# Two attentions and an expert FFN with adaptive norms: projections cut into halves spread over the steps, Newton steps and scaling of the norms moved to GpSimd, a gelu table load set ahead

## Chip, cores and metric

One core of a Trainium2 chip. The metric is the device time in microseconds of one execution of the program. One execution was also profiled; durations, waits and rows below are of that one.

## What is computed

For 8 batches of 512 tokens of 256 features, in float32:

```python
mod = (silu(c) @ wmod).reshape(8, 6, 1, 256)      # sa, ca, ga, sb, cb, gb
ga = sign(ga) * max(|ga|, 0.25); gb = sign(gb) * max(|gb|, 0.25)
h = layernorm(x) * (1 + ca) + sa
x = x + ga * attn(h)          # 16 heads of 16, causal, softmax, output projection
h = layernorm(x) * (1 + cb) + sb
# FFN: xn = layernorm(h) * ln_g + ln_b
#      o = attention(xn)      # 32 heads of 8, not causal, and wo, plus h
#      y = gelu(o_e @ w1[e] + b1[e]) @ w2[e] + b2[e]   # 256 tokens for each of 2 experts a batch
x = x + gb * y
```

## The kernel before, in words

Each batch b passes a first attention (a = 0, 16 heads, causal) and a second one (a = 1, 32 heads, all keys), then two experts (j = 0, 1). A step works on a group of four heads and one tile of 128 keys: 16 steps for the first attention, 32 for the second. In a step (`scores`, L1056) TensorE makes four score tiles of up to 128 x 512, in two pairs, each pair on two halves of its rows; ScalarE takes their exp into `probs` (L852); for the first attention GpSimd sets what the causal mask excludes to zero (L761); then `values` (L1073) multiplies with v into the bank `out`, one step behind. The maxima of the rows come from a second set of the same products, made 8 steps ahead (`maxima`, L1027), reduced by VectorE (L1263 causal, L1266). After four steps of them, `max_rows` turns 16 rows of maxima (L1036), VectorE negates them, GpSimd splits them into three bf16 parts (L743 to L750), and SyncE writes these as extra rows of `q_stack` (L648), so that the score products subtract the maxima themselves. After four steps of values ScalarE copies the sums out (L868), and `normalise` transposes and divides them (L1082, L1286, L1289).

Beside the steps run the other parts of the batches. `layernorm` has three instances: n = 0 of x, n = 1 of x after the first attention, n = 2 of the FFN's input. Each is cut into 17 pieces on VectorE: statistics, twelve small steps of an inverse root on 128 x 4 (`inverse_root`, three of them a first guess, nine Newton steps, L1195 to L1199), and scaling (L1226). `to_features` (L968) transposes into `act_T`. `v` (L1003), `qk` (L990) and `attention_out` (L1118) are projections in float32. A `qk` item fills the bank `side` with 512 tokens; ScalarE copies it as bf16 (L818), VectorE takes the remainder (L1252), GpSimd splits that again (L725, L727), SyncE stores the slices to HBM (L619), and `stacks` loads them as `q_stack` and `k_stack` (L639). `ffn_sum` (L1128) is the second attention's output, `expert_in` (L1147) and `expert_out` (L1163) are the products of an expert, with gelu between (L888). `bias_part` scales the expert's bias and adds it to x for the residual (L795, L800).

The order on each engine is written out by hand. `sections()` gives a list of items for a start, a section before the loop (batch 0 and the first attention of batch 1), a loop of six turns, and a section after it. One turn has 32 steps of the second attention of batch b, then 16 of the first attention of batch b + 2. `attention()` puts the step's own items in a fixed order; every step has four slots, and `beside` maps a slot number to the side items that are put there. In the loop `n1 = 128` is the first slot of the 16 last steps. Each engine walks the same list, in order, and executes its share; a TensorE item that wants a bank waits until its last fill is drained. There are three banks for scores, three for maxima, one `out` and one `side`, which all projections, transposes and turned maxima share.

```python
place_together(beside, (39, 43), v_items(0, 2))
place_together(beside, (47, 51, 55, 59), qk_items(0, 2))
```

So at slot 47 of a turn the items of a whole `qk` product (two products of 512 columns) follow the second pair of step 11.

## Time and profile before

| what | us |
|---|---|
| median of the runs (3) | 1860.25 |
| lowest and highest run | 1859.96, 1870.94 |
| the profiled execution, its own time | 1867.02 |
| its span from first to last instruction | 1865.3 |

The profiled execution is one of its own, 6.8 us above the median. Durations of rows below belong to it. PE is TensorE, PEld its weight loads, DVE VectorE, ACT ScalarE, POOL GpSimd, SP SyncE. A row of a timeline gives start, length, engine, line, instruction, tiles, count, and in brackets the idle time of the engine before it and what ended that. Float32 products are two instructions each in the trace.

### The profile page before, as it was taken

Reading aid. Unit: us, or ns where it says so; the run is one execution under the profiler, and the core shown is the slowest. Engines: PE = TensorE matmul, PEld = TensorE weight load, DVE = VectorE, ACT = ScalarE, POOL = GpSimd, SP = SyncE. Lnnn points to the kernel's source line nnn. Section 1 sums busy time; section 2 is a strip of 40 time slices with the busy share of each in tenths; the row PEclk is TensorE's granted clock in tenths of the full one; section 3 lists DMA queues with packets and bytes.
Section 4 is the critical chain, followed back from the end, with each engine's and each line's share of the span. In section 5 each row is a group of like instructions: output and inputs, shape, how many; then the busy total and the mean of one; then the engine's idle time right before and its main releaser. Section 6 shows DMA issues by size and latency. Waiting matters only on the chain.

```text
span 1865.3 us, 29184 instructions
## 1 busy us (share of the span) xinstructions
PE 1514.1 (81%) x9745; PEld 632.6 (34%) x9745; DVE 1178.4 (63%) x3109; ACT 985.2 (53%) x1967; POOL 447.5 (24%) x797
## 2 busy tenths in 40 slices
PE   4368759898888888898888888898798887878777
PEld 2123213235323353234332353234432353213315
DVE  3456468863786548864687639864688637775440
ACT  0035326664466546664556546664556545566471
POOL 0132422231322222321222312321222312210100
PEclk8679869999999999999999999999999999999999
DMA  6632152342335223442324324342423422121301
GB/s 173 166 109 42 59 146 59 92 128 71 92 100 120 75 68 110 117 126 71 95 84 101 93 72 123 109 117 64 120 66 99 114 72 82 50 78 43 108 1 57
DMA packets 137263, 171.19 MB, mean 92 GB/s; under 512 B 16984, under 2 KB 102808, under 8 KB 137120
## 3 DMA queue, kind: packets, MB, share of 16 engines
q1 hardware_dynamic: 137120, 169.33, 33.1%
q8 instruction: 84, 1.38, 0.3%
q14 instruction: 59, 0.48, 0.1%
HBM read 110.67 MB, written 56.66 MB: 90 GB/s over the span
## 4 chain that ended last, share of the span: by engine, by line
PE 55%; DVE 21%; ACT 8%; DMA 6%; issue 5%; POOL 3%; SPq 2%; POOLq 0%; ACTq 0%; DVEq 0%
DVE neg_max L1266 12%; PE bank_out L1073 11%; PE bank_scores L1056 8%; PE bank_side L990 7%; PE bank_side L1163 7%; PE bank_max L1027 6%; ACT probs L852 4%; PE bank_side L1003 4%; PE bank_side L1147 3%; PE bank_scores L1147 3%; DMA q_stack<-max_parts 2%; PE bank_side L1082 2%; PE bank_side L1128 2%; DMA b_bc<-in_L_ffn_b_dram 1%; DVE normed L1226 1%
## 5 line engine op out<-in xcount | busy, mean ns | idle before, releaser
L852 ACT ACTIVATE probs<-bank_scores 128x512 f32<-128x512 f32 (+3 forms) x1536 | 751.9, 544 | 513.5 <-PE bank_scores L1056 502.4
L1266 DVE TENSOR_REDUCE neg_max<-bank_max 128x1 f32<-128x512 f32 x1024 | 653.4, 682 | 157.0 <-PE bank_max L1027 153.5
L1056 PE MATMUL bank_scores<-q_stack,k_stack 64*128 64x512 bf16 (+3 forms) x2048 | 323.0, 351 | 154.4 <-ACT probs L852 114.1
L1027 PE MATMUL bank_max<-k_stack,q_stack 64*128 64x512 bf16 (+3 forms) x2048 | 324.4, 352 | 97.1 <-DVE neg_max L1266 55.3
L1073 PE MATMUL bank_out<-probs,v_tile 128*9 128x512 f32 (+4 forms) x3072 | 369.7, 554 | 3.7 <-POOL probs L761 1.5
L1263 DVE CUSTOM_DVE_ANT_0 bank_max<-bank_max,causal 128x384 f32<-128x384 f32 (+3 forms) x512 | 241.7, 515 | 124.2 <-PE bank_max L1027 121.1
L1056 PEld LDWEIGHTS bank_scores<-q_stack,k_stack 64*128 64x128 bf16 x2048 | 86.7, 94 | 484.7 <-issue 434.8
L1027 PEld LDWEIGHTS bank_max<-k_stack,q_stack 64*128 64x128 bf16 x2048 | 105.3, 95 | 203.1 <-issue 126.8
L761 POOL TENSOR_SCALAR_AFFINE_SELECT probs<-probs 128x512 f32<-128x512 f32 x128 | 80.9, 632 | 343.7 <-ACT probs L852 343.7
L743 POOL CAST max_parts<-max_row 16x128 bf16<-16x128 f32 x96 | 26.8, 279 | 564.2 <-DVE max_row L1277 564.2
L1163 PE MATMUL bank_side<-w_out,hidden_T 128*128 128x256 f32 x512 | 130.4, 412 | 3.0 <-DVE y_out L1321 1.0
L1321 DVE TENSOR_TENSOR y_out<-bank_side,gb_bc 128x256 f32<-128x256 f32 x32 | 13.6, 425 | 170.9 <-PE bank_side L1163 170.9
L1163 PEld LDWEIGHTS bank_side<-w_out,hidden_T 128*128 128x128 f32 x512 | 102.8, 206 | 37.5 <-DVE max_row L1277 11.0
L1073 PEld LDWEIGHTS bank_out<-probs,v_tile 128*9 128x9 f32 (+1 forms) x3072 | 47.8, 91 | 118.9 <-issue 100.1
L725 POOL CAST partsq<-rest 128x512 bf16<-128x512 f32 x32 | 19.5, 609 | 233.7 <-DVE rest L1252 233.7
L868 ACT ACTIVATE out_raw<-bank_out 128x512 f32<-128x512 f32 x96 | 57.6, 600 | 31.1 <-PE bank_out L1073 30.3
L1003 PE MATMUL bank_side<-wv,act_T 128*128 128x256 f32 x256 | 68.8, 415 | 5.6 <-DVE max_row L1277 2.2
L1263 DVE DVE_READ_ACCUMULATOR2_ANT neg_max<- 128x1 f32 x512 | 72.4, 141 | 0.0
L990 PE MATMUL bank_side<-act_T,wk 128*128 128x512 f32 x128 | 63.5, 618 | 9.1 <-DVE rest L1252 4.0
L990 PE MATMUL bank_side<-act_T,wq 128*128 128x512 f32 x128 | 67.1, 649 | 2.4 <-DVE rest L1252 1.4
L1082 PE MATMUL bank_side<-ident,out_raw 128*128 128x128 f32 x384 | 63.2, 288 | 4.1 <-DVE expert_xT L1314 1.4
L1082 PEld LDWEIGHTS bank_side<-ident,out_raw 128*128 128x128 f32 x384 | 40.8, 142 | 71.0 <-issue 69.4
(113 smaller groups left out, 1405.5 us busy)
## 6 DMA issues: line engine op xcount, KB each, us to landing
q_stack<-q_parts SPq DMA_DIRECT2D x128, 256.0 KB, 4.8
k_stack<-k_parts SPq DMA_DIRECT2D x128, 192.0 KB, 6.7
w_in<-in_L_ffn_w_dram SPq DMA_DIRECT2D x16, 1024.0 KB, 5.8
w_out<-in_L_ffn_w_dram SPq DMA_DIRECT2D x16, 1024.0 KB, 8.2
q_parts<-partsq SPq DMA_DIRECT2D x32, 384.0 KB, 2.6
k_parts<-partsk SPq DMA_DIRECT2D x32, 384.0 KB, 2.6
q_parts<-partsq SPq DMA_DIRECT2D x32, 256.0 KB, 2.9
k_parts<-partsk SPq DMA_DIRECT2D x32, 256.0 KB, 2.9
```

Source lines behind the costliest of these rows:

```text
L761: pool.affine_select(out=tile, in_=tile, compare_op=ALU.is_ge, fill=0.0, base=0, pattern=[[0, GROUP], [1, P]], channel_multiplier=-1).then ...
L852: nc.scalar.activation(probs[s % 2][:, head_at(k), q0:S], region[bank][:, q0:S], ACT.Exp, scale=float(WIDTH[a]) ** -0.5).then_inc(drained[ ...
L990: ins = pe.matmul(region[bank], w_qkv[a][t][:, cc, oc * P:(oc + 1) * P], act_T[:, cc, :], start=(cc == 0), stop=(cc == C - 1))
L1003: ins = pe.matmul(region[bank][:, k * D:(k + 1) * D], act_T[:, cc, t * P:(t + 1) * P], w_qkv[a][2][:, cc, :], start=(cc == 0), stop=(cc == ...
L1027: ins = pe.matmul(region[to][:, 0:keys], q_stack[buf][rows, at, qt * P:(qt + 1) * P], k_stack[buf][rows, at, 0:keys], start=(i == 0), stop ...
L1056: ins = pe.matmul(region[to][:, q0:S], k_stack[buf][rows, at, kt * P:(kt + 1) * P], q_stack[buf][rows, at, q0:S], start=(i == 0), stop=last)
L1073: ins = pe.matmul(outb[32 * k:32 * k + WIDTH[a] + 1, q0:S], v_tile[a][:, kt, g * GROUP + k, :], probs[s % 2][:, k, q0:S], start=(kt == 0), ...
L1082: ins = pe.transpose(side[:, t * P:(t + 1) * P], out_raw[:, g % 2, t * P:(t + 1) * P], ident[:, :])
L1147: ins = pe.matmul(region[bank][:, k * EXP_TOK:(k + 1) * EXP_TOK], w_in[:, cc, ft * P:(ft + 1) * P], expert_xT[:, cc, j * EXP_TOK:(j + 1) * ...
L1163: ins = pe.matmul(region[bank][:, 0:D], hidden_T[:, ft, k * P:(k + 1) * P], w_out[:, ft, :], start=(ft == 0), stop=(ft == FT - 1))
L1263: v.tensor_tensor_reduce(region[bank][:, 0:keys], region[bank][:, 0:keys], causal[:, S - keys:S], 1.0, -3e38, ALU.add, ALU.max, dst).then_ ...
L1266: v.tensor_reduce(dst, region[bank], AX_X, ALU.max).then_inc(drained[bank], 1)
```

## The change

`qk`, `v` and `attention_out` become items of half the size (256 columns of q or k, one tile of 128 tokens of v or of the output), each a fill of `side` of its own, with its copy, remainder, split and add in halves too. In the loop and the section after it they are placed one to a step; in the section before the loop mostly two at one place. Stores to HBM stay whole. VectorE keeps the statistics and the three steps of the first guess; GpSimd does thirteen steps of Newton's method on 128 x 4 (four kinds where VectorE had three, and one that scales by -0.5), and the scaling of 128 x 256 tiles. The copy of the value sums is an item of its own (`sums_out`), half a step later. `bias_part` moves from slot 2 to slot 7. The first `expert_out` item of each expert is placed before the second pair of scores of its step instead of behind it. A new item `gelu_table` computes a gelu of one column, placed ahead of the expert's products. Slots of norms, transposes, stack loads and FFN inputs are moved too.

```diff
-PIECES = {"qk": 2, "v": 2, "attention_out": 2, "ffn_sum": 2, "expert_in": 2, "expert_out": 4}
+PIECES = {"ffn_sum": 2, "expert_in": 2, "expert_out": 4}
...
+            if s % T_STEPS == T_STEPS - 1:
+                half = p * 2 + 2 + VALUES_SLOT[a] // 2 + 1
+                waiting.setdefault((half // 2, half % 2 * 2 + 1), []).append(("sums_out", *main[p]))
...
 def place_experts(plan, off, at):
...
         items = plan.setdefault(start, [])
+        items.append(("gelu_table", off, j))
...
-        place_together(plan, (start + SLOTS, start + 2 * SLOTS), [("expert_out", off, j, k) for k in range(2)])
+        place_at(plan, (start + 2, start + 2 * SLOTS), [("expert_out", off, j, k) for k in range(2)])
...
-    place_layernorm(beside, 82, 0, 1, 4)
+    place_layernorm(beside, 82, 0, 1, 2)
...
-    place_together(beside, (98, 100), v_items(1, 0))
-    place_together(beside, (103, 106, 109, 112), qk_items(1, 0))
+    place_at(beside, (98, 98, 100, 100), v_items(1, 0))
+    place_at(beside, (103, 103, 106, 106, 109, 109, 111, 111), qk_items(1, 0))
...
-    place(beside, 2, [("bias_part", 0, 0), ("bias_columns", 0)])
+    place(beside, 7, [("bias_part", 0, 0), ("bias_columns", 0)])
...
+    place(beside, 12, layernorm_items(2, 0), 2)
+    place_at(beside, (15, 17, 19, 23), out_items(1))
+    place_at(beside, (29, 33), features_items(2, 0))
+    place_at(beside, range(35, 67, 4), qk_items(0, 2))
+    place_at(beside, range(67, 83, 4), v_items(0, 2))
...
+    place(beside, 30, layernorm_items(1, 1), 3)
+    place(beside, 70, layernorm_items(1, 2), 2)
+    place_at(beside, (91, 93), features_items(1, 2))
+    place_at(beside, (95, 97, 99, 103), v_items(1, 1))
+    place_at(beside, range(107, 139, 4), qk_items(1, 1))
...
-    place(beside, n1 + 7, [("stacks", 1, 2), ("keep_v", 1)])
+    place(beside, n1 + 7, [("keep_v", 1)])
+    place(beside, n1 + 18, [("stacks", 1, 2)])
...
+            def layernorm(b, f, n, piece):
+
+                src = (x_in, x1, ffn_x)[n]
+                dst = normed[n % 2]
+                if piece < NEWTON_PIECE:
+                    return
+                if piece == NEWTON_PIECE:
+                    for step in range(GUESS_STEPS, ROOT_STEPS):
+                        newton_step(b, n, step)
+                    return
+                half = piece - NEWTON_PIECE - 1
+                if half == 0:
+                    wait(pool, rstd_made[n], ROOT_STEPS * (b + 1))
+                    for user in ((0, 2), (1,), (0, 2))[n]:
+                        if user in turned_fill:
+                            bank, _ = turned_fill[user]
+                            wait(pool, filled[bank], number(turned_fill[user]) + 1)
+                for t in range(2 * half, 2 * half + 2):
+                    pool.tensor_scalar(dst[:, t, :], src[:, t, :], mean_var[:, n, t, 0:1], rstd[:, n, t:t + 1],
+                                       ALU.subtract, ALU.mult).then_inc(normed_made[n], 1)
+
+            def newton_step(b, n, part):
+
+                a, y, t = root[:, n, 0, :], rstd[:, n, :], root[:, n, 1, :]
+                wait(pool, rstd_made[n], ROOT_STEPS * b + part)
+                if part == GUESS_STEPS:
+                    ins = pool.tensor_scalar(a, a, -0.5, None, ALU.mult)
+                elif part % 4 == 0:
+                    ins = pool.tensor_tensor(t, y, y, ALU.mult)
+                elif part % 4 == 1:
+                    ins = pool.tensor_tensor(t, t, a, ALU.mult)
+                elif part % 4 == 2:
+                    ins = pool.tensor_scalar(t, t, 1.5, None, ALU.add)
+                else:
+                    ins = pool.tensor_tensor(y, t, y, ALU.mult)
+                ins.then_inc(rstd_made[n], 1)
...
+            def gelu_table(b, f, j):
+
+                nc.scalar.activation(spare[:, :], causal[:, 0:1], ACT.Gelu)
...
-            def qk(b, f, a, t, oc, cc):
+            def qk(b, f, a, t, oc, half):
...
+                start_fill(f[0])
+                cols = slice(half * (S // 2), (half + 1) * (S // 2))
                 for cc in range(C):
+                    ins = pe.matmul(region[bank][:, 0:S // 2], w_qkv[a][t][:, cc, oc * P:(oc + 1) * P], act_T[:, cc, cols],
+                                    start=(cc == 0), stop=(cc == C - 1))
+                ins.then_inc(filled[bank], 1)
```

How the order changes on TensorE where a turn of the loop projects q. Before, one step and a half (a row is one product, x2 or x4 how many follow each other; the first numbers are lines of the kernel):

```order
L1073 MATMUL bank_out<-probs,v_tile 9x512 x4
L1056 MATMUL bank_scores<-q_stack,k_stack 128x512 x2
L1027 MATMUL bank_max<-k_stack,q_stack 128x512 x2
L990 MATMUL bank_side<-act_T,wq 128x512 x2
L1056 MATMUL bank_scores<-q_stack,k_stack 128x512 x2
L1027 MATMUL bank_max<-k_stack,q_stack 128x512 x2
L1073 MATMUL bank_out<-probs,v_tile 9x512 x4
L1036 MATMUL bank_side<-ident,neg_max 16x128
L1056 MATMUL bank_scores<-q_stack,k_stack 128x512 x2
L1027 MATMUL bank_max<-k_stack,q_stack 128x512 x2
L990 MATMUL bank_side<-act_T,wk 128x512 x2
```

After, the same place:

```order
L1107 MATMUL bank_scores<-q_stack,k_stack 128x512 x2
L1078 MATMUL bank_max<-k_stack,q_stack 128x512 x2
L1045 MATMUL bank_side<-act_T,wq 128x256 x2
L1107 MATMUL bank_scores<-q_stack,k_stack 128x512 x2
L1078 MATMUL bank_max<-k_stack,q_stack 128x512 x2
L1124 MATMUL bank_out<-probs,v_tile 9x512 x4
L1087 MATMUL bank_side<-ident,neg_max 16x128
L1107 MATMUL bank_scores<-q_stack,k_stack 128x512 x2
L1078 MATMUL bank_max<-k_stack,q_stack 128x512 x2
L1045 MATMUL bank_side<-act_T,wq 128x256 x2
L1107 MATMUL bank_scores<-q_stack,k_stack 128x512 x2
L1078 MATMUL bank_max<-k_stack,q_stack 128x512 x2
```

A whole product of 512 columns gives way to one of 256, and the other half stands in the next step.

TensorE behind the last `expert_in` of an expert, before:

```order
L1027 MATMUL bank_max<-k_stack,q_stack 128x512 x2
L1056 MATMUL bank_scores<-q_stack,k_stack 128x512 x8
L1163 MATMUL bank_side<-w_out,hidden_T 128x256 x8
L1056 MATMUL bank_scores<-q_stack,k_stack 128x384 x4
L1027 MATMUL bank_max<-k_stack,q_stack 128x512 x2
L1036 MATMUL bank_side<-ident,neg_max 16x128
```

And after:

```order
L1078 MATMUL bank_max<-k_stack,q_stack 128x512 x2
L1107 MATMUL bank_scores<-q_stack,k_stack 128x512 x4
L1211 MATMUL bank_side<-w_out,hidden_T 128x256 x8
L1107 MATMUL bank_scores<-q_stack,k_stack 128x512 x4
L1107 MATMUL bank_scores<-q_stack,k_stack 128x384 x4
L1078 MATMUL bank_max<-k_stack,q_stack 128x512 x2
L1087 MATMUL bank_side<-ident,neg_max 16x128
```

The eight products with `hidden_T` stand between the two pairs of scores of a step; behind them the pair of this step and the next one's follow without anything between.

GpSimd at the start of a turn, before (`max_parts` are the parts of the maxima, `x` the residual sum x1):

```order
L748 CAST max_parts<-max_rest 16x128
L750 TENSOR_TENSOR max_parts<-max_rest,max_parts 16x128
L795 TENSOR_TENSOR b_bc<-b_bc,gb_bc 128x256 x2
L800 TENSOR_TENSOR x_res<-x,b_bc 128x256 x4
L743 CAST max_parts<-max_row 16x128
L745 TENSOR_TENSOR max_rest<-max_row,max_parts 16x128
L748 CAST max_parts<-max_rest 16x128
L750 TENSOR_TENSOR max_parts<-max_rest,max_parts 16x128
```

After, from the `x_res` sums to the first half of the Newton steps:

```order
L809 TENSOR_TENSOR x_res<-x,b_bc 128x256 x4
L788 TENSOR_TENSOR x<-x,x_again 128x256 x3
L753 CAST max_parts<-max_row 16x128
L755 TENSOR_TENSOR max_rest<-max_row,max_parts 16x128
L758 CAST max_parts<-max_rest 16x128
L760 TENSOR_TENSOR max_parts<-max_rest,max_parts 16x128
L788 TENSOR_TENSOR x<-x,x_again 128x256
L842 TENSOR_SCALAR root<-root 128x4
L844 TENSOR_TENSOR root<-rstd 128x4
L846 TENSOR_TENSOR root<-root 128x4
L848 TENSOR_SCALAR root<-root 128x4
L850 TENSOR_TENSOR rstd<-root,rstd 128x4
```

The sums `x_res` stand behind the first split instead of ahead of it, and the Newton steps of the next x stand behind the last piece of the residual sum.

## Rows read from the trace of the kernel before

**Rows 1.** The page, part 1: engine, busy us (share of the span), instructions.

```profile
PE 1514.1 (81%) x9745; PEld 632.6 (34%) x9745; DVE 1178.4 (63%) x3109; ACT 985.2 (53%) x1967; POOL 447.5 (24%) x797
```

**Rows 2.** Windows: us, busy us (instructions) of each engine, clock, DMA share, GB/s.

```profile
916.48:1045.96 129.48, 111.88 (x717) 38.45 (x718) 103.26 (x281) 83.23 (x157) 37.55 (x66) 0.99 0.43 115
...
1045.96:1127.89 81.93, 69.54 (x497) 38.22 (x495) 42.05 (x106) 40.08 (x91) 18.18 (x35) 1.00 0.26 69
...
1662.74:1674.75 12.01, 9.57 (x71) 2.44 (x69) 10.88 (x20) 9.17 (x18) 1.39 (x4) 1.00 0.32 78
```

**Rows 3.** Timeline of TensorE in one step: start, us, instruction, count.

```profile
957.29 1.04 PE L1073 MATMUL bank_out<-probs,v_tile 128*9 128x512 f32 x8
...
958.80 1.98 PE L990 MATMUL bank_side<-act_T,wq 128*128 128x512 f32 x4
...
960.72 0.39 PE L1056 MATMUL bank_scores<-q_stack,k_stack 64*128 64x512 bf16 x2
...
961.25 1.05 PE L1073 MATMUL bank_out<-probs,v_tile 128*9 128x512 f32 x8
```

**Rows 4.** Groups of instructions: count | busy us, mean ns | idle before.

```profile
L1195 DVE SCALAR_TENSOR_TENSOR root<-rstd 128x4 f32<-128x4 f32 x72 | 14.7, 203 | 1.0
...
L1197 DVE TENSOR_TENSOR root<-root 128x4 f32<-128x4 f32 x72 | 20.3, 282 | 1.4
...
L1226 DVE TENSOR_SCALAR normed<-x_in,mean_var,rstd 128x256 f32<-128x256 f32 x32 | 11.8, 416 | 0.3
...
L1252 DVE TENSOR_TENSOR rest<-bank_side,partsq 128x512 f32<-128x512 f32 x32 | 22.1, 692 | 62.1 <-ACT partsq L818 62.1
...
L1321 DVE TENSOR_TENSOR y_out<-bank_side,gb_bc 128x256 f32<-128x256 f32 x32 | 13.6, 425 | 170.9 <-PE bank_side L1163 170.9
...
L852 ACT ACTIVATE probs<-bank_scores 128x256 f32<-128x256 f32 x128 | 42.1, 382 | 98.6 <-PE bank_scores L1056 98.6
```

**Rows 5.** Groups of instructions on GpSimd.

```profile
L745 POOL TENSOR_TENSOR max_rest<-max_row,max_parts 16x128 f32<-16x128 f32 x96 | 40.1, 417 | 7.8
...
L768 POOL TENSOR_TENSOR normed<-normed,mod_bc 128x256 f32<-128x256 f32 x32 | 22.7, 725 | 9.8 <-DVE normed L1226 9.8
```

**Rows 6.** Timeline at the start of a turn.

```profile
917.45 2.78 POOL L800 TENSOR_TENSOR x_res<-x,b_bc 128x256 f32<-128x256 f32 x4
...
918.30 2.54 DVE L1266 TENSOR_REDUCE neg_max<-bank_max 128x1 f32<-128x512 f32 x4
...
927.95 0.39 PE L1056 MATMUL bank_scores<-q_stack,k_stack 64*128 64x512 bf16 x2 [2.68 <-DMA q_stack<-max_parts]
```

**Rows 7.** Timeline round the first expert of a turn.

```profile
1069.17 1.28 ACT L888 ACT_TABLE_LOAD   x1
...
1071.65 0.84 ACT L888 ACTIVATE hidden_T<-bank_side,b_cur 128x256 f32<-128x256 f32 x2 [1.20 <-PE bank_side L1147]
...
1079.30 1.28 ACT L852 ACT_TABLE_LOAD   x1 [0.77 <-PE bank_scores L1056]
...
1081.34 0.61 PE L1056 MATMUL bank_scores<-q_stack,k_stack 64*128 64x512 bf16 x4 [2.10 <-ACT probs L852]
...
1081.88 3.72 PE L1163 MATMUL bank_side<-w_out,hidden_T 128*128 128x256 f32 x16
```

**Rows 8.** Groups of instructions: the copy of the value sums.

```profile
L868 ACT ACTIVATE out_raw<-bank_out 128x512 f32<-128x512 f32 x96 | 57.6, 600 | 31.1 <-PE bank_out L1073 30.3
```

**Rows 9.** The page, part 6: DMAs, KB each, median us to landing.

```profile
k_stack<-k_parts SPq DMA_DIRECT2D x128, 192.0 KB, 6.7
```

**Rows 10.** Timeline of the first products of q and k.

```profile
52.32 0.60 ACT L818 ACTIVATE partsq<-bank_side 128x512 bf16<-128x512 f32 x1 [2.80 <-PE bank_side L990]
...
53.69 1.99 PE L990 MATMUL bank_side<-act_T,wk 128*128 128x512 f32 x4 [1.41 <-DVE rest L1252]
```

**Rows 11.** Timeline: transpose behind the second norm, first section.

```profile
205.50 0.80 PE L968 MATMUL bank_side<-ident,normed 128*128 128x128 f32 x4 [2.25 <-DVE normed L1226]
```

**Rows 12.** One line's instructions: min/median/max ns, first and last start.

```profile
L1197 DVE TENSOR_TENSOR root<-root x72: 143/163/820, 7.9 to 1600.9; 128x4 f32<-128x4 f32 x72
```

230 lines of the change are left out of this document (100 added, 130 removed).

## Prediction

> **What bounds the kernel now.** I read the page first, then the windows over one turn of the loop, then timelines inside it. The page shows no engine full: TensorE is busy 81% of the span, VectorE 63% [rows 1]. The windows split one turn (the fourth, some 211 us) in two [rows 2]. In the 32 steps of the second attention (129.48 us, 4.05 a step) TensorE is busy 111.88, VectorE 103.26, ScalarE 83.23; in the 16 steps of the first attention, which carry the experts (81.93 us), 69.54, 42.05 and 40.08. So TensorE is the nearest bound, and it is idle because work comes in lumps. Two timelines show the lump. A step with a whole projection takes 3.96 us, and TensorE runs without a hole: values with a pair of scores and of maxima 1.51, the projection 1.92, the second pair 0.53 [rows 3]. Four steps with no projection take 12.01 us, 3.00 each: VectorE 10.88 busy, TensorE only 9.57 [rows 2], so there VectorE's four maxima set the pace. 14 of the 32 steps are of the first kind, lengthened to 4.1 to 5.1 by transposes. Each kind leaves the other engine waiting.
>
> **Halves of projections.** The work on TensorE is the same: a projection of 512 columns is 4 instructions in 1.98 us [rows 3], and 16 of 256 columns, twice a projection's worth, took 3.72 [rows 7]. After the change the 32 steps hold 26 pieces of about 1 us and two more lie in the steps behind. The sum for the stretch: TensorE 111.9 - 2 = 110 us. VectorE loses, for each of three norms, nine Newton steps (two kinds have rows, the third I take as the first: 3 x (2 x 0.203 + 0.282) = 2.06 us) and four scalings (4 x 0.416 = 1.66), 11.2 in all [rows 4]; it gains 14 x 0.425 - 8 x 0.692 = 0.4 for the remainders of q and k and 4 x 0.425 - 2 x 0.692 = 0.3 for the output projection: 103.3 - 10.5 = 93. ScalarE pays twice 0.382 where it paid 0.60 once [rows 4, 10], 2 us more. TensorE is then the one bound. How full can it run? Both ends are in the rows: 100% in the 3.96 us step, 86% over the stretch as it is (111.88/129.48), and the engine that sets the pace in the light steps reaches 10.88/12.01 = 91%. I take 95%, nearer the steps in which TensorE leads: 110/0.95 = 116 us, 13.5 less. Ends: 91% gives 121 (-8.5), 98% gives 112 (-17).
>
> **Norms on GpSimd.** Its small operations are not in the trace on 4 elements. Bounds: a tensor_tensor on 16 x 128 took 0.417 with 0.08 of idle behind its own semaphore (7.8 us / 96) [rows 5], so at most 0.50 a step; VectorE's 0.203 is the lower end. From 128x256 to 16x128 the time falls from 0.725 to 0.417 [rows 5], that is 0.31 for 128 elements, which leaves 0.11 and the wait: I take 0.25. 13 steps: 3.3 us (2.6 to 6.5). A scaling of 256 elements lies between 0.42 and 0.725; I take 0.5, 2.0 for four. A norm is thus ready 5.3 us after its guess (4.3 to 9.4), where VectorE needed 3.6. Who waits? In the loop the norm of the next x has its Newton steps behind the fourth piece of the output projection in GpSimd's queue; from that piece to the transpose on TensorE there are about 1.4 steps, some 4.5 us, against 0.43 + 0.73 + 5.3 = 6.5. That is a new stall of 2 us a turn (1 to 6). Behind the norm on GpSimd stand the parts of the next row of maxima; they have three steps of slack. The other two norms of a turn have ten slots or more and I count them at nothing.
>
> **Bias work behind the maxima's parts.** At the start of a turn GpSimd first waits for a gate load, then adds x_res (2.78 us), and only then, at 920.2, splits the row of maxima that VectorE had finished before 918.30; TensorE later waits 2.68 us for the patch of q_stack made from it [rows 6]. Moved to slot 7, this work stands behind the split: 1.8 us earlier. The wait that remains (1 us) is the transfer's own time; the gain is part of the idle counted above.
>
> **Expert output moved between two pairs of scores.** In the trace TensorE waits 2.10 us for scores banks, since ScalarE loads the exp table (1.28 us) before the first exp; only then come 3.72 us of expert output [rows 7]. Placed before the second pair, those products hide the load. Then the next step's pair needs a bank that the second pair has just filled, about 0.5 us until its exp. Net 1.5 us, twice a batch, seven batches: 21 us, three a turn.
>
> **Gelu table.** This edit does not do what it says. The load already runs from 1069.17 to 1070.45, beside the products, and the first gelu then waits for TensorE until 1071.65 [rows 7]: of the 1.20 us of idle left there, the new one-element activation takes some 0.2. Cost and gain 0; without that cover it would cost 0.2 a load. The Trainium skill (ScalarE: Activation LUTs, Table-load gate) says that a load is placed right before the activation that needs it, and that the first call is slow for it. Were the first gelu to pay it, hiding the 1.28 us under the products would bring 15 x 1.28 = 19 us; the trace does not bear this out, since the load does not wait as the activation does.
>
> **Copies of the value sums half a step later.** ScalarE stood 30.3 us before them [rows 8], in front of exps that were ready. TensorE feels this only where scores banks run out; 0.5 us a turn.
>
> **Stack loads of the next second attention.** They leave 11 slots later, since the last q and k pieces now fall into the first attention. Their first reader comes 13 slots, some 11 us, behind; a load lands in 6.7 [rows 9] after waiting on SyncE for the last slices to be stored, some 3. Slack 1 to 2 us: cost 0, at worst 2 a turn. The parts of a row of maxima stand behind them on SyncE and share that slack.
>
> **The turn.** Second attention -13.5 + 2 = -11.5; first attention -3 - 0.5 + 1.5 (two more pieces on TensorE) = -2. Together -13.5, six turns: -81.
>
> **Last section.** 16 pieces instead of 8 wholes, in a stretch where TensorE and VectorE are equally busy and two loads of the stacks are waited for as before: -5; experts -3; the two norms there have six slots to their transposes: +1. Sum -7.
>
> **First section.** Here pieces stand in pairs, and there is one side bank. From the end of a qk product to the next one 1.40 us pass, copy 0.60 and remainder 0.69 among them [rows 4, 10]; with halves 1.40 - 0.21 - 0.27 = 0.93, but twice as often. At the start 8 x 0.93 - 4 x 1.40, with four v pieces 0.5 more, and the last split 0.8 shorter: +1.5. Ten pairs later: four of qk at 0.95, four of v at 0.5, two of output at 0.55, less one such wait already there: +6.5. The chain x1, norm, scaling by ln, second norm, transposes is on TensorE's path here (it waited 2.25 us for the last scaling [rows 11]); GpSimd's two norms put 2 x 1.7 on it and the first scaling no longer overlaps the multiplies of GpSimd, 2.6: +6. Spread qk of the second batch and the sums: -3. Sum +11.
>
> **Total.** -81 - 7 + 11 = -77. The profiled execution took 1867.02 us around a span of 1865.3; that gives 1790. It stands 6.8 us above the median of the runs shown, 1860.25, so on that scale 1783. Of terms without a row of their own (fill of TensorE above all) I trust the smaller half more and say 1786.
>
> **Rivals.**
> GpSimd too slow, and the kernel slower. Every microsecond of a norm beyond 5.3 is paid where TensorE waits for the next x, and beyond 7 also at the last norm of a turn: 2 us a turn, 4 in the outer sections, 16 in all. 77 us are used up when a norm takes about 11 us, that is at some 0.6 us a Newton step with 0.725 for a scaling. At 0.75 a step (12.7 us): 16 x 7.4 - 11 - 77 = +30, time 1890. For it: VectorE's tensor_tensor on 4 elements took 0.163 at the median but up to 0.820 [rows 12]: something holds it at times, and GpSimd's operations may. Against it: four 128x256 adds on GpSimd took 2.78 us (0.70 each, 0.725 is their mean) while VectorE's reductions ran at 0.64 each [rows 5, 6]. The Trainium skill (GPSIMD Engine Reference, Specifications) says that GpSimd's SBUF interface is shared with VectorE and contended by instructions with two SBUF inputs; by that rule this rival bites beside such instructions and not beside the reductions, and both rows agree. Chance 0.06.
> Halves bring nothing, since each piece needs a round trip through ScalarE and VectorE and the light steps beside them keep the pace that they have. Left are the experts (-21), 1.8 x 7 = -12 for the split, and +11: -22, time 1838. For it: the light steps stand at 3.00 though VectorE is busy for 2.72. Against: the 3.96 us step runs full. Chance 0.13.
> TensorE at 98% and no norm waited for: 129.5 to 112, -17.5 - 2 a turn, -117 - 8 + 8 = -117: 1743. Chance 0.10. Between this and no change in sign lies my own case, chance 0.71: its terms give 8.5 - 6 + 2 = 4.5 to 19 a turn, -27 to -114.
>
> **How the numbers follow.** I forecast 1786 us. The range 1750 to 1833 leaves out most of the best case, the worst, and part of the second rival. A measurement of this kernel can tell about 1% from no change (18.6 us). Faster by more: 0.71 and 0.10 and most of 0.13 less the weak end of my case: 0.88. Within 1%: 0.06. Slower: 0.06.
>
> **What would show it.** Right: second-attention stretch near 117 us with TensorE above 93% and steps of 3.4 to 3.8 us; no 2.1 us wait before expert output, and one near 0.5 behind it; q_stack waits at a turn's start near 1 us; gelu loads as before; GpSimd steps of root near 0.25. Wrong: transposes of normed (bank_side<-ident,normed) waiting more than 5 us a turn; steps still alternating; the first section, to the loop's start, not longer.

## The result and the profile after

The changed kernel takes 1889.96 us (median of four runs, 1888.70 to 1891.57) against 1860.15 for the kernel before: ratio 1.0146, 95% interval 1.0109 to 1.0184. It is 1.5% slower; 1786 was forecast. The profiled execution took 1888.70 us around a span of 1887.0.

The page's first part, after (answers to [rows 1]):

```profile
PE 1530.2 (81%) x10001; PEld 661.4 (35%) x10001; DVE 1135.7 (60%) x2877; ACT 1006.9 (53%) x2079; POOL 651.8 (35%) x1349
```

VectorE did lose its work (1178 to 1136 us), GpSimd got 204 us more, and TensorE's share is 81% as before. Cut at the first product with values of each attention, the span of the profiled execution divides so ("a turn" is the mean of the six, "median us" that of all runs):

| kernel | median us | ratio to before | to the loop | 32 steps, mean | 16 steps, mean | a turn | last section |
|---|---|---|---|---|---|---|---|
| before | 1860.15 | | 273.0 | 129.7 | 83.8 | 213.5 | 311.3 |
| changed | 1889.96 | 1.0146 | 298.9 | 130.0 | 82.1 | 212.0 | 315.9 |

Of the 21.7 us by which the span grew, 25.9 lie ahead of the loop and 4.6 behind it; six turns gave back 9. (The medians differ by 29.8, so these spans show the change some 8 us too mildly.) So the gain of the 32 steps, -13.5 in the forecast, is missing entirely. Windows over the fourth turn, with [rows 2] beside them:

```profile
936.23:1065.77 129.54, 113.30 (x745) 41.62 (x746) 96.75 (x249) 84.24 (x166) 62.21 (x132) 0.96 0.40 105
1065.77:1147.82 82.05, 70.76 (x502) 38.96 (x500) 43.59 (x108) 41.80 (x95) 18.67 (x36) 1.00 0.29 86
```

The 32 steps are as long as before (129.48) although VectorE's busy time fell from 103.26 to 96.75. TensorE's rose by 1.4 us, at a lower mean clock. Where it stood is told by the page's groups:

```profile
L1022 PE MATMUL bank_side<-ident,normed 128*128 128x128 f32 x192 | 40.2, 346 | 87.3 <-POOL normed L834 76.1
```

And the groups of GpSimd's instructions (count | busy us, mean ns | idle before), which answer to [rows 4, 5]:

```profile
L834 POOL TENSOR_SCALAR normed<-x_in,mean_var,rstd 128x256 f32<-128x256 f32 x32 | 38.7, 1222 | 0.9
...
L848 POOL TENSOR_SCALAR root<-root 128x4 f32<-128x4 f32 x72 | 16.0, 222 | 6.4
...
L844 POOL TENSOR_TENSOR root<-rstd 128x4 f32<-128x4 f32 x72 | 14.3, 199 | 5.8
```

TensorE waited 76.1 us for scaled tiles, 15 times. One scaling takes 1.22 us on GpSimd. The forecast had 0.5, and 0.725 as its upper end [rows 5]. A Newton step takes 0.20 to 0.22, with 0.08 of wait behind its own semaphore. The timeline of the fourth turn shows one such wait and what follows it:

```profile
957.36 0.24 POOL L842 TENSOR_SCALAR root<-root 128x4 f32<-128x4 f32 x1
...
961.15 4.84 POOL L834 TENSOR_SCALAR normed<-x_in,mean_var,rstd 128x256 f32<-128x256 f32 x4
```

```profile
959.58 1.05 PE L1124 MATMUL bank_out<-probs,v_tile 128*9 128x512 f32 x8
966.13 1.09 PE L1022 MATMUL bank_side<-ident,normed 128*128 128x128 f32 x4 [5.50 <-POOL normed L834]
...
969.60 1.80 PE L1124 MATMUL bank_out<-probs,v_tile 128*9 128x512 f32 x8
971.33 0.66 PE L1022 MATMUL bank_side<-ident,normed 128*128 128x128 f32 x4
```

Thirteen steps from 957.36 to 961.15 are 3.79 us, four scalings 4.84: a norm takes 8.6 us from its guess. TensorE stands for 5.50 us and then works at half rate until about 971: the same transposes take 1.09 and then 0.66, the same products with values 1.05, 1.80. The second wait of the turn is for the last norm:

```profile
1014.72 0.24 POOL L842 TENSOR_SCALAR root<-root 128x4 f32<-128x4 f32 x1 [6.56 <-DVE rstd L1235]
...
1018.59 0.28 POOL L753 CAST max_parts<-max_row 16x128 bf16<-16x128 f32 x1 [0.18 <-DVE max_row L1307]
...
1020.20 4.83 POOL L834 TENSOR_SCALAR normed<-normed,mean_var,rstd 128x256 f32<-128x256 f32 x4
```

```profile
1025.18 0.63 PE L1022 MATMUL bank_side<-ident,normed 128*128 128x128 f32 x4 [3.07 <-POOL normed L834]
```

Here the split of a row of maxima stands between the Newton steps and the scalings, and the norm takes 10.3 us from its guess.

### The profile page after: what moved, and what is told of

Read it like the earlier page. It is cut to its first block, busy times and chain, and to the rows that moved or that the text cites. A ratio compares the mean times of both kernels' runs of the same rounds, so it can differ in the third digit from the quotient of the medians.

```text
span 1887.0 us, 30243 instructions
## 1 busy us (share of the span) xinstructions
PE 1530.2 (81%) x10001; PEld 661.4 (35%) x10001; DVE 1135.7 (60%) x2877; ACT 1006.9 (53%) x2079; POOL 651.8 (35%) x1349
## 3 DMA queue, kind: packets, MB, share of 16 engines
q8 instruction: 86, 1.41, 0.3%
## 4 chain that ended last, share of the span: by engine, by line
PE 63%; DVE 11%; ACT 8%; POOL 7%; issue 5%; DMA 3%; SPq 2%; POOLq 0%; ACTq 0%
PE bank_out L1124 15%; PE bank_scores L1107 10%; PE bank_max L1078 7%; PE bank_side L1045 7%; PE bank_side L1211 6%; DVE neg_max L1296 5%; ACT probs L904 4%; POOL normed L834 4%; PE bank_side L1055 4%; PE bank_side L1195 3%; PE bank_scores L1195 3%; PE bank_side L1133 2%; PE bank_side L1022 2%; PE bank_side L1176 2%; PE bank_side L1167 2%
## 5 line engine op out<-in xcount | busy, mean ns | idle before, releaser
L1124 PE MATMUL bank_out<-probs,v_tile 128*9 128x512 f32 (+4 forms) x3072 | 378.7, 566 | 21.9 <-ACT out_raw L918 12.9
L1211 PE MATMUL bank_side<-w_out,hidden_T 128*128 128x256 f32 x512 | 118.8, 385 | 4.8 <-issue 2.8
L1022 PE MATMUL bank_side<-ident,normed 128*128 128x128 f32 x192 | 40.2, 346 | 87.3 <-POOL normed L834 76.1
L1211 PEld LDWEIGHTS bank_side<-w_out,hidden_T 128*128 128x128 f32 x512 | 94.6, 190 | 35.0 <-DVE max_row L1307 11.1
L735 POOL CAST partsq<-rest 128x256 bf16<-128x256 f32 x64 | 25.4, 396 | 200.4 <-DVE rest L1282 200.4
L1055 PE MATMUL bank_side<-wv,act_T 128*128 128x256 f32 x256 | 76.9, 425 | 9.5 <-ACT v_tile L878 2.4
L1045 PE MATMUL bank_side<-act_T,wk 128*128 128x256 f32 x256 | 76.1, 422 | 10.1 <-DVE rest L1282 7.4
L1045 PE MATMUL bank_side<-act_T,wq 128*128 128x256 f32 x256 | 75.1, 417 | 9.9 <-DVE rest L1282 5.3
L1022 PEld LDWEIGHTS bank_side<-ident,normed 128*128 128x128 f32 x192 | 26.4, 174 | 131.6 <-issue 125.3
```

The costliest lines, as they stand in the source:

```text
L1022: ins = pe.transpose(region[bank][:, t * P:(t + 1) * P], src[:, t, cc * P:(cc + 1) * P], ident[:, :])
L1045: ins = pe.matmul(region[bank][:, 0:S // 2], w_qkv[a][t][:, cc, oc * P:(oc + 1) * P], act_T[:, cc, cols], start=(cc == 0), stop=(cc == C - 1))
L1055: ins = pe.matmul(region[bank][:, 0:D], act_T[:, cc, t * P:(t + 1) * P], w_qkv[a][2][:, cc, :], start=(cc == 0), stop=(cc == C - 1))
L1124: ins = pe.matmul(outb[32 * k:32 * k + WIDTH[a] + 1, q0:S], v_tile[a][:, kt, g * GROUP + k, :], probs[s % 2][:, k, q0:S], start=(kt == 0), ...
L1211: ins = pe.matmul(region[bank][:, 0:D], hidden_T[:, ft, k * P:(k + 1) * P], w_out[:, ft, :], start=(ft == 0), stop=(ft == FT - 1))
```

## The experiments

Each row's ratio is to runs of the kernel before on the same chip, which took 1860.15 to 1864.58 us there; a difference of 4 us between rows of two chips shows nothing. Sections are of the profiled execution, as in the table above.

| label | median us | ratio (95% interval) | to the loop | 32 steps | 16 steps | a turn | last |
|---|---|---|---|---|---|---|---|
| norm_only | 1894.78 | 1.0161 (1.0127 to 1.0194) | 281.1 | 132.2 | 83.7 | 215.9 | 317.3 |
| expert_only | 1840.19 | 0.9870 (0.9834 to 0.9905) | 268.7 | 129.8 | 79.4 | 209.2 | 313.2 |
| norm_dve | 1840.73 | 0.9872 (0.9851 to 0.9893) | 289.7 | 124.3 | 82.1 | 206.4 | 308.0 |
| scale_dve | 1871.14 | 1.0049 (1.0025 to 1.0072) | 290.6 | 128.5 | 82.1 | 210.5 | 314.7 |
| norm_early | 1844.91 | 0.9896 (0.9874 to 0.9917) | 299.5 | 122.2 | 82.1 | 204.3 | 318.8 |
| whole_first | 1836.49 | 0.9846 (0.9803 to 0.9888) | 292.6 | 122.9 | 82.1 | 205.0 | 317.1 |
| sums_back | 1825.05 | 0.9787 (0.9743 to 0.9830) | 299.7 | 120.7 | 80.9 | 201.6 | 313.6 |
| halves_dve | 1827.42 | 0.9805 (0.9782 to 0.9828) | 289.1 | 124.1 | 80.9 | 205.0 | 308.1 |
| no_table | 1825.76 | 0.9797 (0.9774 to 0.9819) | 298.0 | 120.4 | 80.9 | 201.3 | 319.4 |
| copy_apart | 1805.46 | 0.9698 (0.9669 to 0.9728) | 296.5 | 117.9 | 80.9 | 198.8 | 313.7 |
| best | 1786.13 | 0.9591 (0.9562 to 0.9620) | 279.4 | 117.9 | 80.9 | 198.8 | 310.4 |
| best_dve | 1804.76 | 0.9684 (0.9656 to 0.9711) | 276.9 | 122.1 | 80.9 | 203.0 | 309.7 |
| best_whole | 1815.62 | 0.9759 (0.9729 to 0.9790) | 278.7 | 122.1 | 82.1 | 204.2 | 310.7 |

The outer sections of one execution are rough. The stretch ahead of the loop is the same program in before (273.0) and expert_only (268.7), and no_table differs from sums_back by 5.8 us in the last section, though only the gelu table parts them. Less than some 6 us in one of these columns is not shown by it.

**The norms.** Four kernels ask whether GpSimd's norms are what cost, and whether by their length or by their place.

norm_dve (all of a norm on VectorE, its nine Newton steps in slots of their own and the pieces of a norm closer together; the rest as changed):

```diff
-ROOT_STEPS = GUESS_STEPS + 1 + 4 * NEWTON
+ROOT_STEPS = 3 + 3 * NEWTON
...
-            walk(pool, {"layernorm": layernorm, "to_features": to_features, "qk": qk, "max_rows": max_rows, "scores": scores, "ffn_input": ffn_input, "bias_part": bias_part,
+            walk(pool, {"qk": qk, "max_rows": max_rows, "scores": scores, "ffn_input": ffn_input, "bias_part": bias_part,
...
-                    first_guess(b, n, piece - 3)
+                    inverse_root(b, n, piece - 3)
```

> The changed kernel with all of the norm work back on VectorE (nine Newton steps and the scaling, spread over slots as in the kernel before); halves, expert output, gelu table and every other slot as changed. Theory A (GpSimd's scaling of 1.22 us a tile makes a norm 8.6 us long; TensorE waits for it twice a turn and runs at half clock behind each wait; the halves gained what was forecast): some 11 us a turn less than the changed kernel, 66 in the loop, 20 in the outer sections: about 1804. Theory B (halves and the rest bring little, the holes only change their name and go to VectorE): not more than 25 less, 1865 or above.

Measured 1840.73: 49 us less than the changed kernel, not 86. The norms are the largest loss, but with them gone the 32 steps are 5.4 us shorter than before's, not 13.5, and the section ahead of the loop is still 16.7 longer. Something else is lost.

norm_early (both norms of a turn earlier, GpSimd keeps them):

```diff
-    place(beside, 12, layernorm_items(2, 0), 2)
+    place(beside, 9, layernorm_items(2, 0))
...
-    place(beside, 70, layernorm_items(1, 2), 2)
+    place(beside, 70, layernorm_items(1, 2))
```

> The changed kernel with both norms as they are, on GpSimd, but the first norm of a turn placed from slot 9 on, one piece a slot (before: from slot 12, one every second slot), and the last one from slot 70, one piece a slot (before: every second slot). Outer sections unchanged. Theory A: both waits of the loop for normed vanish, 11 us a turn, about 1823. Theory B (GpSimd's work contends with VectorE or blocks the splits of maxima wherever it stands): 1870 or more.

1844.91, 45 less; 7.7 of the forecast 11 us a turn. In the loop the norms' place was wrong, not their engine as such.

scale_dve (Newton steps on GpSimd, scaling on VectorE):

```diff
+                    for t in range(2 * half, 2 * half + 2):
+                        v.tensor_scalar(dst[:, t, :], src[:, t, :], mean_var[:, n, t, 0:1], rstd[:, n, t:t + 1],
+                                        ALU.subtract, ALU.mult).then_inc(normed_made[n], 1)
```

> The changed kernel with only the scaling (four instructions a norm) back on VectorE; the thirteen Newton steps stay on GpSimd. Theory A: a norm takes 3.8 + 1.7 = 5.5 us instead of 8.6, the wait for the first norm of a turn falls from 5.5 to about 2.4 and that for the last vanishes: 8 us a turn less, 1825 to 1830; VectorE waits for GpSimd's steps now and then. If instead the number of Newton steps (13 with a semaphore each) is what costs, it stays above 1865.

1871.14: a miss. It lies above 1865, where the expectation put it if the thirteen Newton steps are what costs; no run changed their number, so their share stays open. VectorE now waits for GpSimd's root with its own maxima queued behind. The waits of the whole program show it:

```profile
DVE normed L1252 <- POOL rstd L839: 38.7, 18, 5.0
PE bank_side L1011 <- DVE normed L1252: 34.0, 9, 8.4
```

Columns: total us, times, longest. With the norm split between two engines, VectorE waits 38.7 us for the root and TensorE still 34.0 for scaled tiles, where TensorE alone waited 76.1. That the wait on VectorE then costs through the maxima is argued, not shown.

norm_only (the kernel before, norms alone moved):

```diff
+                if piece == 6:
+                    for step in range(GUESS_STEPS, ROOT_STEPS):
+                        newton_step(b, n, step)
```

> The kernel before with the norm change alone: Newton steps and scaling on GpSimd, in that kernel's own slots, whole projections, everything else as before. Theory A: TensorE waits some 3 us for normed at both norms of a turn, with half clock behind it, 6 to 8 us a turn; with 15 in the first section 1860 + 57 = 1917. Theory B: within 1% of 1860.

1894.78, 31 us slower than before, not 57. TensorE waited 44.4 us for `normed`. So the move alone, in the old slots, is a loss. In the changed kernel it costs 49 (norm_dve) and TensorE waits 76.1; whether that is the halves or the other slots no run parts.

**What a scaling costs on GpSimd.** micro adds 48 single operations at the start of the kernel before.

```diff
+                        if n == 0:
+                            ins = pool.tensor_scalar(d, a, p0, p1, ALU.subtract, ALU.mult)
+                        elif n == 1:
+                            ins = pool.tensor_scalar(d, a, p0, None, ALU.subtract)
...
```

> The kernel before with 48 single GpSimd operations added at its start, each twice behind its own semaphore, on 128 partitions and 4, 64, 128 and 256 elements: tensor_scalar with two per-partition operands (the scaling's form), with one, with two constants, with one constant, tensor_tensor, and a copy. What makes a scaling take 1.22 us where an add of two tiles takes 0.73? Theory A1: the second operation (subtract, then multiply) is a second pass: the form with two constants costs as much, the ones with one operation half. Theory A2: the per-partition operands are fetched at each use: the forms with operands cost more than those with constants on 4 elements already. Of the whole time nothing is read.

Groups of GpSimd's instructions, the mean of the two of each form; L726 is the scaling's form, L728 one operand per partition, L730 two constants, L732 one constant, L734 tensor_tensor, L736 a copy:

```profile
L726 POOL TENSOR_SCALAR mic<-mic 128x256 f32<-128x256 f32 x2 | 2.9, 1455 | 0.2
L730 POOL TENSOR_SCALAR mic<-mic 128x256 f32<-128x256 f32 x2 | 2.1, 1072 | 0.2
L728 POOL TENSOR_SCALAR mic<-mic 128x256 f32<-128x256 f32 x2 | 1.8, 920 | 0.2
L732 POOL TENSOR_SCALAR mic<-mic 128x256 f32<-128x256 f32 x2 | 1.8, 916 | 0.2
...
L734 POOL TENSOR_TENSOR mic<-mic 128x256 f32<-128x256 f32 x2 | 1.2, 613 | 0.2
...
L726 POOL TENSOR_SCALAR mic<-mic 128x4 f32<-128x4 f32 x2 | 0.8, 384 | 0.2
...
L732 POOL TENSOR_SCALAR mic<-mic 128x4 f32<-128x4 f32 x2 | 0.5, 229 | 0.2
L734 POOL TENSOR_TENSOR mic<-mic 128x4 f32<-128x4 f32 x2 | 0.4, 200 | 0.2
```

Neither theory holds in full. A second operation adds 0.16 us on 256 elements (1.07 against 0.92), so it is no second pass. Two operands add 0.15 on 4 elements. The surprise is the form itself: tensor_scalar with one constant takes 0.92 where tensor_tensor, which reads a tile more, takes 0.61. From 4 to 256 elements that is 2.7 ns an element against 1.6 ((916 - 229)/252; (613 - 200)/252). An add could not bound a scaling. Of the two scalings of 256 elements the first took 1.70, the second the 1.22 of the changed kernel.

**The expert output.** expert_only, on the kernel before:

```diff
-        place_together(plan, (start + SLOTS, start + 2 * SLOTS), [("expert_out", off, j, k) for k in range(2)])
+        place_together(plan, (start + 2, start + 2 * SLOTS), [("expert_out", off, j, k) for k in range(2)])
```

> The kernel before with only the first expert_out item of each expert moved ahead of the second pair of scores of its step. By the term of the prediction 1.5 us an expert, 14 experts: 21 us faster, 1840. Rival: the wait of 2.1 us is exchanged for one of the same size a step later (the next pair needs the bank filled last): within 5 us of 1860.

1840.19, 22 us less than the kernel before on that chip (18 to 31 by the interval of the ratio), where 21 was forecast. In the changed kernel the new place looks so:

```profile
1099.63 0.61 PE L1107 MATMUL bank_scores<-q_stack,k_stack 64*128 64x512 bf16 x4 [0.66 <-issue]
1100.17 3.72 PE L1211 MATMUL bank_side<-w_out,hidden_T 128*128 128x256 f32 x16
1103.82 0.61 PE L1107 MATMUL bank_scores<-q_stack,k_stack 64*128 64x512 bf16 x4
1105.21 0.50 PE L1107 MATMUL bank_scores<-q_stack,k_stack 64*128 64x384 bf16 x4 [0.78 <-ACT probs L904]
```

The wait of 2.10 us [rows 7] is gone, one of 0.78 is left behind. The 16 steps take 79.4 us against 83.8 in the mean, but that is two gains. Windows over the 16 steps of the first, second and fourth turn before, and of the first of expert_only:

```profile
401.26:486.39 85.13, 72.75 (x497) 40.12 (x496) 42.05 (x106) 40.09 (x91) 17.83 (x34) 0.96 0.24 66
617.50:701.08 83.58, 71.20 (x498) 39.11 (x496) 42.05 (x106) 40.08 (x91) 17.38 (x33) 0.98 0.23 62
1045.96:1127.89 81.93, 69.54 (x497) 38.22 (x495) 42.05 (x106) 40.08 (x91) 18.18 (x35) 1.00 0.26 69
```

```profile
396.94:476.38 79.44, 69.54 (x498) 38.22 (x496) 42.05 (x106) 40.11 (x91) 17.75 (x34) 1.00 0.26 70
```

Where the granted clock stayed at full the gain is 2.5 us a turn, near the two waits of 2.10 less the 0.78 left behind each. In the other five turns before, TensorE worked at half rate behind one or both of these waits (2.10 and 2.17 us), at 1.6 us each. In the first turn the clock gave way here, and the expert's products took 5.41 us instead of 3.72:

```profile
436.64 0.61 PE L1056 MATMUL bank_scores<-q_stack,k_stack 64*128 64x512 bf16 x4 [2.10 <-ACT probs L852]
437.18 5.41 PE L1163 MATMUL bank_side<-w_out,hidden_T 128*128 128x256 f32 x16
```

In expert_only all six turns are at full clock there. With this, norm_dve at the same 1841 says that all the rest of the change, without GpSimd's norms, adds up to nothing.

**The copy of the value sums.** sums_back, on norm_early:

```diff
-            if s % T_STEPS == T_STEPS - 1:
-                half = p * 2 + 2 + VALUES_SLOT[a] // 2 + 1
-                waiting.setdefault((half // 2, half % 2 * 2 + 1), []).append(("sums_out", *main[p]))
```

> The version with the earlier norms (label norm_early) with the copy of the value sums back where the kernel before has it, right behind the values. Theory: the later copy makes TensorE wait for the bank of the sums (1.2 us at a turn's first values, 12.9 us in all in the changed kernel, with half clock behind some of them), so this is 2 to 3 us a turn and 15 to 20 in all faster, 1828. Rival: the copy stands again in front of exps that are ready, as in the kernel before, and costs as much: within 5 of 1845.

1825.05, 20 us faster, 1.2 us in the 16 steps and 1.5 in the 32. In the changed kernel's timeline a turn begins with

```profile
936.23 1.05 PE L1124 MATMUL bank_out<-probs,v_tile 128*9 128x512 f32 x8 [1.23 <-ACT out_raw L918]
```

The bank is handed back half a step later, and TensorE's next values are already there. ScalarE's idle time in front of this copy [rows 8], 30.3 us, fell to 1.2 and was worth less than what it cost TensorE: 12.9 us of waiting for the bank in the changed kernel, none in sums_back.

halves_dve is the same step on norm_dve:

```diff
+            def values(b, f, a, s):
+                if s % T != T - 1:
+                    return
```

> The changed kernel with all norm work on VectorE (as norm_dve) and with the copy of the value sums back behind the values. What is left of the change are the halves, the expert output between the pairs, the gelu table, the bias work at slot 7 and the slots. Theory: as against norm_dve it gains what sums_back gained, 20: 1821; so against the kernel before with the expert output moved (1840) the halves and slots are worth 20 net of 17 lost ahead of the loop. Rival: with VectorE loaded by the norms the earlier copy gains nothing: 1840.

1827.42 against 1840.73, on another chip: 13 of the 20 expected, 1.4 us a turn of it.

**Two small copies beside GpSimd.** copy_apart, on sums_back:

```diff
-    place(beside, 7, [("bias_part", 0, 0), ("bias_columns", 0)])
+    place(beside, 2, [("bias_columns", 0)])
+    place(beside, 7, [("bias_part", 0, 0)])
```

> The version with earlier norms and the copy of the value sums back (label sums_back), and VectorE's two copies of the expert's bias columns (128x8) back at slot 2 of a turn, GpSimd's part of that work staying at slot 7. In the changed kernel the two copies took 2.17 us, from 941.52 to the end of GpSimd's four adds at 943.59, and TensorE then waited 1.73 us for maxima; the copies took 0.45 at slot 2. Theory: the copies are held while GpSimd runs tensor_tensor; 2 to 4 us a turn with the clock behind it, 12 to 25 in all, 1805. Rival: the wait is VectorE's normalising work, not the copies: within 4 of 1825.

1805.46, as expected: 20 us less than sums_back, 2.8 of it in each turn. The rows of the changed kernel, VectorE and GpSimd at the start of the fourth turn, then TensorE:

```profile
940.83 2.76 POOL L809 TENSOR_TENSOR x_res<-x,b_bc 128x256 f32<-128x256 f32 x4
...
941.52 2.17 DVE L1336 COPY b_cur<-b_T 128x8 f32<-128x8 f32 x2
...
944.43 0.39 PE L1078 MATMUL bank_max<-k_stack,q_stack 64*128 64x512 bf16 x2 [1.73 <-DVE neg_max L1296]
```

One copy of 128x8 begins at 941.52 and the pair ends at 943.69, just behind GpSimd's adds (943.59). The line's own rows, of the changed kernel and of copy_apart (least, median and largest ns):

```profile
L1336 DVE COPY b_cur<-b_T x16: 157/162/2107, 305.6 to 1779.7; 128x8 f32<-128x8 f32 x16
```

```profile
L1337 DVE COPY b_cur<-b_T x16: 159/161/166, 296.3 to 1696.4; 128x8 f32<-128x8 f32 x16
```

The median hides how regular this is: in the changed kernel the first copy of seven of the eight pairs was held, for 1.67 us once and for 2.10 to 2.11 six times, each time to the end of the adds. The eighth pair had no GpSimd work beside it. In copy_apart, where none of the 16 has, no copy takes more than 0.166 us. By the Trainium skill (GPSIMD Engine Reference, Specifications) the two engines share an SBUF interface, with contention for VectorE instructions that run in a two-port mode or have two SBUF inputs. The rows agree that the engines collide, while reductions of the maxima beside such adds kept 0.64 each [rows 6]; the copy has one SBUF input, and whether it ran in a two-port mode no row shows.

**The gelu table.** no_table, on sums_back:

```diff
-        items.append(("gelu_table", off, j))
```

> The version sums_back without the early gelu of one column. By the prediction's term (the table load lies under the products either way) within 4 of 1825. Rival (the first gelu pays for the load): 15 to 19 us slower, 1842.

1825.76 against 1825.05 (ratio to before 0.9797, interval 0.9774 to 0.9819): nothing, as the term had it.

**The sections outside the loop.** whole_first, on norm_early:

```diff
-    before += v_items(0, 0) + qk_items(0, 0)
+    before += v_items(0, 0) + whole_qk(0, 0)
...
-    place_at(beside, range(1, 17, 2), qk_items(0, 1))
+    place_at(beside, (1, 5, 9, 13), whole_qk(0, 1))
```

> The version with the earlier norms with whole q and k products in the start and in the section before the loop (at the slots that the kernel before has), halves in the loop and behind it. Theory: back-to-back halves leave 0.93 us of idle behind 1.13 of work and the clock falls to half speed (2.07 us a piece from the fourth on), where wholes ran at full speed; with the ten later pairs this explains most of the 17 us by which the first section of norm_dve is longer than before's: some 14 us faster than norm_early, 1831. Rival: the first section is set by the norms and the stack loads, and the halves only fill their waits: under 5 us.

1836.49: 8 us faster of the 14 expected; 6.9 of it ahead of the loop. Three of before's four whole products ran at full rate with 1.41 us between them [rows 10]. The changed kernel's timeline at the same place:

```profile
50.90 1.13 PE L1045 MATMUL bank_side<-act_T,wq 128*128 128x256 f32 x4 [0.93 <-DVE rest L1282]
52.96 2.07 PE L1045 MATMUL bank_side<-act_T,wq 128*128 128x256 f32 x4 [0.93 <-DVE rest L1282]
55.97 2.08 PE L1045 MATMUL bank_side<-act_T,wk 128*128 128x256 f32 x4 [0.93 <-DVE rest L1282]
```

From the fourth q piece on a half takes longer (2.07) than a whole took (1.99). The clock has gone to its lower level, 1.2 of 2.4 GHz; over 50 to 100 us the windows give it as 0.53 of full (0.62 before):

```profile
50.00:100.00 50.00, 21.77 (x81) 9.94 (x81) 17.24 (x67) 2.69 (x7) 15.38 (x34) 0.53 0.62 155
```

best joins what the runs favoured; the new part is where the outer norms run:

```diff
+        def on_vector(b, n):
+            return b == 0 or b == (BATCHES - 1 if n else 1)
```

> What the runs so far favour, together: halves in the loop and behind it, whole q and k products in the start and ahead of the loop, norms earlier and on GpSimd in the loop, on VectorE in both outer sections, value sums copied at once, bias columns copied at slot 2. If the parts add up: 1825 - 17 (copies) - 7 (wholes) - 9 (first section's norms) - 5 (last section's) = 1787. If they overlap: 1800 to 1810.

1786.13: the parts add up. It is 4.1% faster than the kernel before and 5.5% faster than the changed one. Windows over its fourth turn:

```profile
876.44:993.64 117.20, 109.74 (x745) 41.24 (x746) 96.43 (x251) 86.13 (x168) 62.22 (x132) 1.00 0.45 121
993.64:1074.53 80.89, 70.59 (x501) 38.98 (x499) 42.46 (x107) 40.91 (x94) 18.73 (x36) 1.00 0.27 80
```

TensorE is busy 109.74 of 117.20 us, 94%, at full clock. From the changed kernel the way down is 45 us (the norms earlier), 20 (the copy of the value sums), 20 (the bias columns) and 19 (whole products and VectorE's norms in the outer sections): 104, as much as the forecast missed. That best itself takes the 1786 us of the forecast is chance: it has whole products and VectorE's norms where the change has neither.

best_dve is best with all norms on VectorE; best_whole is best with whole q and k products in the loop as well:

```diff
-    place_at(beside, range(35, 67, 4), qk_items(0, 2))
+    place_at(beside, range(39, 71, 8), whole_qk(0, 2))
...
-    place_at(beside, range(107, 139, 4), qk_items(1, 1))
+    place_at(beside, range(111, 143, 8), whole_qk(1, 1))
```

> As best, but all norm work on VectorE (nine Newton steps and scaling, spread over the slots as in norm_dve). Is the move to GpSimd worth anything once its norms are placed early enough? Theory: VectorE gets 7 us a turn back that fill holes beside maxima; norm_early with the sums and norm_dve with the sums differ by 2.4 us in all, of which the outer sections take 10 the other way: some 12 to 20 slower than best, 1800. Rival: VectorE isn't the bound in the loop and the norms are worth nothing there: within 5 of 1786.

> As best, but with whole q and k products in the loop too, one every second step (4 for the first attention, 4 for the second one); v and output products stay in halves, all else as in best. This prices the halves of q and k alone, with the hindrances gone. Theory (the halves fill TensorE as forecast, most of the 13.5 us of a stretch with two thirds of the pieces): 6 to 9 us a turn, 1822 to 1840. Rival (what best gains comes from the norms, the copies and the expert output, halves are nothing): within 6 of 1786.

1804.76 and 1815.62. Placed right, the norms on GpSimd gain 4.2 us a turn, all of it in the 32 steps; the halves of q and k gain 5.4 us a turn, 4.2 of it in the 32 steps. best_whole fell short of what was expected of it: 6 to 9 us a turn, 1822 to 1840.

## Why the prediction was wrong

**Halves, -13.5 a turn.** The term joins the halves and the norms' leaving VectorE. It came nearly true once nothing else stood in the way: 117.9 us in copy_apart and best for the 32 steps, where 116 was forecast, at 94% fill where 95% was (VectorE came down to 96.4 us, not 93). Of the 11.8 us by which that is shorter than before, the halves of q and k are 4.2 and GpSimd's norms 4.2; the other 3.4 (halves of v and of the output, the earlier split) were not taken apart. But the forecast summed the change as it stood, and there it was 130.0: other terms ate it.

**Norms on GpSimd.** This is the step that failed most: "A scaling of 256 elements lies between 0.42 and 0.725; I take 0.5, 2.0 for four." It took 1.22, 4.84 for four. The upper end was an add's, an operation of another form, and VectorE's ratio (0.416 against its own adds) was no guide. The Newton steps, 3.3 us forecast, took 3.79, and fell inside the bounds. A norm of 8.6 us, against 5.3, still lay inside the stated 4.3 to 9.4, but only because the upper end for the small steps was loose. It was waited for twice a turn: 5.50 us where 2 was forecast (1 to 6), and 3.07 at the last norm where nothing was. The two together pass the forecast's own sign of being wrong, more than 5 us a turn. The forecast's "the other two norms of a turn have ten slots or more and I count them at nothing" failed too: from GpSimd's first Newton step at slot 82 (1014.72) to where TensorE stood at the transposes of slot 91 (1022.11) there were 7.4 us for a norm that took 10.3 with the maxima's split inside it. norm_early took back 45 us of this, and 8 more lie ahead of the loop (norm_only, 281.1 against 273.0; +6 was forecast).

**The first rival** (GpSimd too slow) is the one that came true, with chance 0.06 and the time it gave. The agreement in time is luck: 1890 stood there for a norm of 12.7 us against a gain of 77 for all the rest, and neither came. Its price for a norm was near: 16 us for each microsecond beyond 5.3, less 11, makes 42 at 8.6, and norm_dve puts 49 on the norms, waits, half rate behind them and masks together. What was wrong is the 77 on the other side, which the terms below took away.

**Copies of the value sums.** Forecast 0.5 us a turn gained; measured 2.7 a turn lost (sums_back). The forecast looked at ScalarE's wait and not at who waits for the bank.

**Bias work.** The gain of an earlier split was seen: the wait for `q_stack` at the start of the fourth turn, 2.68 us before [rows 6], is 1.15 in copy_apart, where some 1 us was forecast; in the changed kernel it is gone. But the step went by what GpSimd does and left out that VectorE's two copies moved with it. copy_apart puts 20 us on it. The trace of before had the sign of it, and it was not read: the same 16 copies took 0.164 us at the median and 0.744 at most, beside GpSimd's multiplications (there the copy ended with one of them, while GpSimd went on). The rule on the shared interface was weighed against the norms alone, and not against VectorE's copies.

**First section, +11.** It was +25.9: 16.7 without the norms (norm_dve), where +5 was forecast. Wholes take back 7 of it beside GpSimd's norms and 12 beside VectorE's (halves_dve 289.1, best_dve 276.9, the copies moved too). The term for the start took the halves at full rate; five of the eight of q and k ran at half. Ahead of the loop GpSimd's scaling also stood before the causal masks; TensorE waited 5.65 us for one at 207.97. What is left of the 16.7, 4 us, is no more than such sections differ by themselves.

**Last section, -7.** It was +4.6. The forecast gave the two norms there +1. GpSimd's norm and the multiplications behind it (1601.66 to 1611.99) stood in front of the split of a row of maxima, and TensorE waited for both:

```profile
1616.35 0.61 PE L1107 MATMUL bank_scores<-q_stack,k_stack 64*128 64x512 bf16 x2 [5.70 <-DMA q_stack<-max_parts]
...
1629.43 1.09 PE L1022 MATMUL bank_side<-ident,normed 128*128 128x128 f32 x4 [6.22 <-POOL normed L834]
```

Neither wait is in norm_dve, whose last section is 308.0 us.

**Right:** the expert output (-21; 22 measured, though part of it is the clock: 2.5 us a turn by the wait, where 3 was forecast, and 1.9 by full rate behind it), the gelu table (0), and TensorE's work in the stretch (110; 109.7). The last section without the norms (308.0 against 311.3, where -8 was forecast) is too near to its own spread to count.

**No term at all** stood for the clock, though the kernel before already paid for it, 1.6 us behind a wait of 2.10. Behind the waits of 5.50 and 3.07 us TensorE worked at half rate for about 5 and 3 us: in the fourth turn 113.30 us busy instead of best's 109.74.

## What to carry to other kernels

When work moves to another engine, price every form of instruction there by a row of that same form, or measure it alone first; a neighbour's row is not an upper bound. Then move the placement with the price: the same norms cost 34 us in the loop in one slot (changed against norm_dve) and gained 25 in another, one to three steps earlier and with the other hindrances gone (best against best_dve). An item moved for one engine's sake moves on all engines that share in it: list who else executes it and what runs beside it at the new place.

## What the runs showed of the hardware

- GpSimd's tensor_scalar on 128x256 f32 takes 0.92 us with one constant, 1.07 with two operations, 1.22 with two operations and per-partition operands in the running kernel; tensor_tensor 0.61 alone and 0.73 in the kernel.
- A 128x8 copy on VectorE took up to 2.107 us where GpSimd ran four tensor_tensor adds (1.67 to 2.11 in seven of seven), 0.16 with no GpSimd work beside it; reductions beside such adds did not lengthen.
- Waits of 2.10 and 2.17 us on TensorE at the experts left the granted clock at full in one turn and were followed by products at half rate in others; each time that cost 1.6 us (16 steps of 81.93, 83.58 and 85.13 us at 1.00, 0.98 and 0.96 of the clock).
- Back-to-back fills of 1.13 us with 0.93 idle between them let TensorE fall to half rate at the fourth; fills of 1.99 with 1.41 between did not at that place. In the loop the same kind of hole went either way: one of 2.41 us (norm_early, fourth turn) left the clock up, one of 1.96 (fifth turn) was followed by products at half rate. Why was not tried.
